# Transformer block of an audio tower on one core: all of W_o's tiles on two-part operands, biases in row groups, two more blocks split

## The reference, cut to what matters

```
h = patches @ W.T + b                        # 64 batches x 10 positions = 640 tokens, D = 512
n = layernorm(h)
q, k, v = n @ Wq.T, n @ Wk.T, n @ Wv.T       # 16 heads of 32, rotary angles on q and k
scores  = q k^T / sqrt(32), causal
heavy   = the key with the largest column sum of softmax(scores)
probs   = softmax(scores where key is heavy or |i - j| <= 1)
h = h + (probs v) @ Wo.T
n = layernorm(h)
h = h + (silu(n @ Wg.T) * (n @ Wu.T)) @ Wd.T # inner width 2048
```

## Time and profile before

| | us |
|---|---|
| median of three runs | 273.25 |
| lowest, highest | 272.64, 273.52 |
| profiled execution, its own time | 272.49 |
| its span, first to last instruction | 270.4 |
| TensorE busy, weight loads busy | 260.1, 215.0 |
| VectorE, ScalarE, GpSimd busy | 169.9, 103.6, 60.0 |

### The profile page before, as it was taken

The page is one execution under the profiler, slowest core; times in us unless marked ns, Lnnn a source line. Parts: engine busy times, 40 slices in busy tenths (PEclk is TensorE's granted clock), DMA queues, the critical chain, the costliest instruction groups (busy, mean ns, idle before and its releaser), DMA issues.

```text
span 270.4 us, 4977 instructions
## 1 busy us (share of the span) xinstructions
PE 260.1 (96%) x1893; PEld 215.0 (80%) x1893; DVE 169.9 (63%) x326; ACT 103.6 (38%) x174; POOL 60.0 (22%) x49
## 2 busy tenths in 40 slices
PE   7999999999899999999989999999999999999993
PEld 5465388893787878687778888999999999999992
DVE  1676998898879976799993864633333333333323
ACT  2211122650274463659531053644333433334320
POOL 0104000002063622103900101322333222222210
PEclk9999999999999999999999999999999999999999
DMA  6995030000048999984493041495333333300004
GB/s 212 421 414 190 15 119 2 2 2 0 0 138 178 327 248 276 281 259 165 152 235 119 1 136 60 123 341 161 116 118 116 116 116 116 127 28 0 0 0 116
DMA packets 12578, 37.51 MB, mean 139 GB/s; under 512 B 1616, under 2 KB 1616, under 8 KB 11920
## 3 DMA queue, kind: packets, MB, share of 16 engines
q1 hardware_dynamic: 11120, 32.15, 34.8%
q0 software_dynamic: 1152, 4.72, 9.2%
q10 hardware_dynamic: 288, 0.39, 0.4%
HBM read 31.23 MB, written 1.31 MB: 120 GB/s over the span
## 4 chain that ended last, share of the span: by engine, by line
PE 68%; DVE 19%; issue 6%; ACT 2%; DMA 2%; POOL 1%; SPq 1%; DVEq 0%; POOLq 0%
PE ps L221 45%; PE ps L1281 5%; PE ps L1300 5%; DVE prod L249 4%; PE ps L1195 3%; PE ps L1103 3%; DVE stats L673 2%; DMA dims<-w_dims 2%; PE ps L1156 1%; PE ps L1125 1%; PE ps L1054 1%; DVE pr L811 1%; PE ps L1135 1%; DVE rowv L809 1%; DVE gu L917 1%
## 5 line engine op out<-in xcount | busy, mean ns | idle before, releaser
L221 PE MATMUL ps<-xT,wgu 128*128 128x384 f32 x384 | 70.5, 339 | 0.1
L221 PEld LDWEIGHTS ps<-xT,wgu 128*128 128x128 f32 x384 | 68.1, 188 | 1.7 <-issue 0.5
L917 DVE TENSOR_TENSOR gu<-silu,ps 128x256 f32<-128x256 f32 (+1 forms) x32 | 15.5, 484 | 50.5 <-PE ps L221 44.4
L358 POOL TENSOR_TENSOR wd<-stage,wd 128x512 fp32r<-128x512 f32 x16 | 26.2, 1637 | 77.1 <-ACT wd L433 77.1
L221 PE MATMUL ps<-wd,hT 128*128 128x512 f32 x156 | 38.8, 393 | 0.0
L572 ACT ACTIVATE silu<-ps 128x256 f32<-128x256 f32 (+1 forms) x32 | 14.1, 440 | 54.5 <-PE ps L221 49.9
L221 PEld LDWEIGHTS ps<-wd,hT 128*128 128x128 f32 x156 | 29.0, 188 | 5.4
L433 ACT ACTIVATE wgu<-stage 128x1024 fp32r<-128x1024 f32 x20 | 21.1, 1056 | 24.0 <-PE ps L221 23.1
L221 PEld LDWEIGHTS ps<-xs,wgu 128*128 128x128 f32 x216 | 25.8, 188 | 3.4 <-issue 1.9
L221 PE MATMUL ps<-xs,wgu 128*128 128x256 f32 x216 | 28.0, 286 | 0.0
L1300 PE MATMUL ps<-stage,gu 128*128 128x512 f32 x56 | 26.5, 595 | 1.2 <-DVE gu L917 1.2
(11 more groups left out here) (122 smaller groups left out, 331.1 us busy)
## 6 DMA issues: line engine op xcount, KB each, us to landing
stage<-w_ffn SPq DMA_DIRECT2D x32, 512.0 KB, 4.3
stage<-w_ffn SPq DMA_DIRECT2D x32, 256.0 KB, 3.7
wgu<-stage POOLq DMA_DIRECT2D x5, 512.0 KB, 7.8
stage<-w_k SPq DMA_DIRECT2D x1, 1024.0 KB, 7.0
stage<-w_q SPq DMA_DIRECT2D x1, 1024.0 KB, 10.5
stage<-w_v SPq DMA_DIRECT2D x1, 1024.0 KB, 12.5
wo<-w_o SPq DMA_DIRECT2D x1, 1024.0 KB, 14.0
wd<-stage POOLq DMA_DIRECT2D x2, 512.0 KB, 7.4
```

The costliest lines, as they stand in the source:

```text
L221: ins = pe.matmul(dst, lhs[a], rhs[b], start=first and n == 0, stop=last and n == 2)
L358: pool.tensor_tensor(dst, src, f32(hi), ALU.subtract).then_inc(done, 1)
L917: dve.tensor_tensor(gu[:, ring, cols], silu[:, ring, cols], ps[:, up, at:at + P * TILES[p]], ALU.mult)\
```

## The change

W_o is loaded into slot 3 of `stage` and split right after the embedding; block 3's load waits until the adding DMA of W_o has landed. The attention of units 0 and 1 gets a low part too (`low_attn(0)`, `low_attn(1)` on VectorE), and `project_out` uses `mm3` for all tiles. `S1` becomes 2, so blocks 2 and 3 of the first pass are split, `hi_whole` and `low_whole` move forward, and `minus_weights(2)` and `(3)` stand around `hi_attn(0)` and `(1)`. The biases of v of group 0 and of all of group 1 are added by products with 8 rows in three row groups (`project_biases`); three GpSimd DMAs for each matrix copy the bias rows there (`spread_bias`). The causal mask goes into one more row of the `place` product, and ScalarE copies the result (`place` on ScalarE). k's third part is projected and rotated later, bias products are moved apart from the tokens they belong to, position 9's reduction is cut in two, the masked softmax has its parts at 4 to 9 and 0 to 3 in place of 0 to 7 and 8 and 9, W_v's bias product is cut in two pieces around `score_place(0)`, v of group 1 is projected between the value sums, and `spread_scale(1)` stands behind the transposes of tile 0. Memory is laid out anew, which adds no instruction.

```diff
-S1, S2 = 4, 11
+S1, S2 = 2, 11
# SP
-            sp.dma_start(wo[:, :, :].rearrange("p k n -> p (k n)"), w_o).then_inc(dma_wo, 16)
+            sp.dma_start(stage[:, 3, :], w_o).then_inc(dma_wo, 16)
...
-            gate_up_load(3)
-            down_load(3)
-            for x in range(3):
+            for x in range(2):
                 sp.wait_ge(fold_bias_mm, x + 1)
                 gate_up_load(x)
                 down_load(x)
+            sp.wait_ge(fold_bias_mm, 3)
+            gate_up_load(2)
+            down_load(2)
+            sp.wait_ge(dma_wo_low, 16)
+            gate_up_load(3)
+            down_load(3)
# GpSimd
+            def spread_bias(x):
+                pool.wait_ge(fold_bias_set, x + 1)
+                for n in range(len(PARTS)):
+                    pool.dma_start(spread[GB * n:GB * n + 2 * NQ, x], fold_bias[0:P:GB // 2, x]).then_inc(dma_spread[x], 16)
...
             key_add(0)
             key_add(1)
+            spread_bias(0)
             key_add(2)
+            spread_bias(1)
+            low_wo()
+            spread_bias(2)
             power(3)
             power(4)
+            low_weights(2)
             power(LN2[1])
+            low_weights(3)
             power(LN2[0])
...
-            low_wo()
# ScalarE
+            def place(n):
+                a, b = CHUNKS[n]
+                act.wait_ge(place_mm, n + 1)
+                if n == 0:
+                    act.wait_ge(sums_set, 2)
+                act.activation(sm[:, a:b].rearrange("p i h j -> p (i h j)"), ps[:, SCORE_BANK[n], 0:HQ * NPOS * (b - a)], ACT.Copy)\
+                   .then_inc(placed, 1)
...
+            folded(2)
             embedded(3)
             embedded(4)
-            folded(2)
-            folded_bias(2)
+            minus_wo()
             chunk_out(0)
+            place(0)
             exponential(0)
             chunk_out(1)
+            place(1)
+            folded_bias(2)
             exponential(1)
...
             act.activation(warm[:, :], neghalf[:, :], ACT.Silu)
+            minus_weights(2)
             hi_attn(0)
             hi_attn(1)
+            minus_weights(3)
             whole_tokens(1)
             whole_tokens(0)
+            hi_whole()
             drain(("v", 1, 0))
-            drain(("v", 1, 1))
-            drain(("v", 1, 2))
# VectorE
             rotate("k", 1)
-            rotate("k", 2)
             bias_join(1)
...
+            rotate("k", 2)
             rotate("q", 2)
             early_products(8)
             early_products(9)
+            dve.wait_ge(product_set, NPOS)
+            step(last_scores(0, 5))
+            softmax_in(0)
+            step(last_scores(5, NPOS))
+            softmax_out(0)
+            softmax_in(1)
             bias_join(2)
-            place(0)
-            softmax_in(0)
-            dve.wait_ge(product_set, NPOS)
-            step(score_reduce(9))
-            softmax_out(0)
-            place(1)
-            softmax_in(1)
             softmax_out(1)
             heavy_keys()
             softmax_in(2)
             softmax_in(3)
             softmax_out(2)
-            values(0, 7, 6, 5, 4, 3, 2, 1, 0)
+            values(0, 7, 6, 5, 4)
             softmax_out(3)
+            low_attn(0)
+            values(0, 3, 2, 1, 0)
             statistics(3)
             statistics(4)
-            token_scale(3)
-            token_scale(4)
+            low_attn(1)
             statistics(LN2[1])
             normalise(LN2[1])
             statistics(LN2[0])
+            token_scale(3)
+            token_scale(4)
             normalise(LN2[0])
             tables(1)
             turn("k", 0)
...
             turn("q", 0)
             first_pass(0)
+            low_whole()
             first_pass(1)
# TensorE
+            def project_biases(x, g):
+                m = "kqv".index(x)
+                pe.wait_ge(pick_set, 1)
+                pe.wait_ge(dma_spread[m], 16 * len(PARTS))
+                for n, (a, b) in enumerate(PARTS):
+                    rows = slice(GB * n, GB * n + 2 * NQ)
+                    dst = ps[:, PROJECT_BANK[PROJECT.index((x, g, n))], 0:DH * (b - a)].rearrange("p (i n) -> p i n", n=DH)
+                    pe.matmul(dst, pick[rows, :], repeated(spread[rows, m], 1, b - a), start=False, stop=True).then_inc(project_mm, 1)
...
+            score_sums(0, ("projection", ("q", 0, 0)))
+            fold_weight_bias(2, 0, 1)
+            score_place(0, ("projection", ("q", 0, 1)))
+            score_sums(1, ("projection", ("k", 0, 2)))
+            fold_weight_bias(2, 2, 3)
+            score_place(1, ("projection", ("q", 0, 2)))
+            project_tokens(("v", 0, 0), ("fold", 2))
+            project_tokens(("v", 0, 1), ("embedding", 3))
+            project_tokens(("v", 0, 2), ("embedding", 4))
+            project_tokens(("k", 1, 0), ("chunk", 0))
+            project_tokens(("k", 1, 1), ("chunk", 1))
+            project_biases("v", 0)
+            project_tokens(("k", 1, 2), ("scores", 0))
+            project_biases("k", 1)
...
+            project_biases("q", 1)
+
+            value_sums(0, ("projection", ("k", 1, 2)))
+            project_tokens(("v", 1, 0), ("fold bias", 2))
+            project_out(1, 1, ("projection", ("k", 1, 0)))
+            value_sums(1, ("projection", ("q", 1, 0)))
+            project_tokens(("v", 1, 1), ("projection", ("v", 0, 2)))
+            project_tokens(("v", 1, 2), ("projection", ("k", 1, 1))).then_inc(tokens_mm, 1)
             project_out(0, 2, ("projection", ("q", 1, 2)))
...
             transposes(LN2[1], ("wo", 1))
-            read_out("projection", ("k", 1, 0))
-            pe.wait_ge(apart_set, NT)
-            spread_scale(1)
+            project_biases("v", 1)
             pe.wait_ge(xf_sb, 1)
             gate_up_whole(0, 1)
             gate_up_whole(1, 1)
             transposes(LN2[0], ("wo", 0))
+            read_out("projection", ("q", 1, 1))
+            pe.wait_ge(apart_set, NT)
+            spread_scale(1)
             pe.wait_ge(xf_sb, 2)
```

More of the change, by code:

```diff
@@ L41 @@
 BIG = 3.4028234663852886e38
+LOWEST = 2.0 ** 127
 CUTS = {"ident": P, "cos": NPOS * HD, "sin": NPOS * HD, "band": NPOS * NPOS, "rank": NPOS, "batch": P, "quad": NQ,
-        "causal": NPOS * NPOS, "quarter": P, "low": 1, "sign": 1, "place": 9 * HQ * NPOS}
+        "quarter": P, "pick": P, "low": 1, "sign": 1, "place": 9 * HQ * NPOS}
 CONSTS = sum(CUTS.values())
@@ L51 @@
 PARTS = [(0, 4), (4, 8), (8, 10)]
-PROJECT = [(x, g, n) for g in range(NG) for x in "kqv" for n in range(len(PARTS))]
-ROTATE = [item for item in PROJECT if item[0] != "v" and item[1] == 0]
+ROTATE = [("k", 0, 0), ("k", 0, 1), ("q", 0, 0), ("q", 0, 1), ("k", 0, 2), ("q", 0, 2)]
+PROJECT = ROTATE + [(x, g, n) for x, g in (("v", 0), ("k", 1), ("q", 1), ("v", 1)) for n in range(len(PARTS))]
 DRAIN = [item for item in PROJECT if item not in ROTATE]
@@ L190, in audio_tower @@
         bias_high, bias_low = sem("bias_high"), sem("bias_low")
+        pick_set, sums_set, dma_spread = sem("pick_set"), sem("sums_set"), [sem(f"dma_spread{n}") for n in range(3)]
         mean_mm, centred_set = sem("mean_mm"), sem("centred_set")
@@ L835, in mask, with low_attn @@
                 step(dve.tensor_tensor(rows(sm, part), rows(sm, part), rows(keep, part), ALU.min))
+            def low_attn(u):
+                a, b = UNITS[u][2]
+                dve.wait_ge(attn_sb, u + 1)
+                dve.tensor_tensor(xT[:, 1, :, columns(u)], ps[:, UNIT_BANK[u], :].rearrange("p (k n) -> p k n", k=KT)[:, :, GB * a:GB * b],
+                                  f32(xT[:, 0, :, columns(u)]), ALU.subtract).then_inc(attn_lo, 1)
             def values(g, *queries):
@@ L978, in _ @@
             scores(1, 3)
-            low_whole()
             turn("q", 1)
@@ L1104, in fold_weight, with fold_weight_bias @@
                 ins.then_inc(fold_mm, 1)
+            def fold_weight_bias(x, *chunks):
                 if x:
                     read_out("fold bias", x - 1)
-                for k in range(KT):
+                for k in chunks:
                     for q in range(NQ):
@@ L1144, in project_parts @@
                     project_tokens((x, g, n), last[n])
-                for n in range(len(PARTS)):
-                    project_bias((x, g, n))
+                project_biases(x, g)
             def score_sums(n, last):
@@ L1165, in score_place @@
                 pe.wait_ge(chunk_sb, n + 1)
-                pe.matmul(ps[:, SCORE_BANK[n], 0:HQ * NPOS * (b - a)], sums[0:rows, n],
-                          cut["place"][0:rows, HQ * NPOS * a:HQ * NPOS * b], start=True, stop=True).then_inc(place_mm, 1)
+                pe.matmul(ps[:, SCORE_BANK[n], 0:HQ * NPOS * (b - a)], sums[0:rows + 1, n],
+                          cut["place"][0:rows + 1, HQ * NPOS * a:HQ * NPOS * b], start=True, stop=True).then_inc(place_mm, 1)
             def spread_scale(g):
@@ L1225, in _ @@
             fold_weight(0)
-            project(("k", 0, 0))
-            project(("k", 0, 1))
```

(11 more changed lines are left out.)

148 lines of the change are left out of this document (65 added, 83 removed).

## The result

The changed kernel takes **277.89 us** (median of four runs, 276.99 to 279.10), the kernel before 273.38 beside it (272.64 to 273.79): a ratio of 1.0172, with a 95% interval of 1.0146 to 1.0199. It is 4.5 us slower where 2.5 were forecast, inside the range given.

What follows compares the result with a forecast made beforehand. TensorE was taken as the bound between 44 and 68 us, with VectorE having 2.6 us to spare. Terms +0.65 + 1.6 + 1.65 - 1.4 = +2.5 us on 273.25 gave 275.8 us, range 272.6 to 278.6.

Steps and rivals of the forecast that it cites:

- Up to the second score product: TensorE up to `score_place(1)`: filled waits and fewer changes between kinds of product make it 1.25 us early.
- The bias copies: First bias triple of v: TensorE waits 1.4 us (0 to 4.5) for GpSimd's DMAs, losing most of the early gain.
- Whatever the size: GpSimd's DMA issue: its instruction takes 0.87 us at any size, so each bias copy was given 0.87.
- The low parts of the attention: Attention to transposes of tile 1: 1.35 us are lost, leaving the second layernorm and normalised tile late by 0.65.
- The tables: Group 1's tables, up to `down_whole(0)`: the later `spread_scale(1)` costs 1.6 us more, making `down_whole(0)` late by 2.25.
- The split of the tokens: `low_whole` ahead of pass 2: GpSimd's value products hold it, about 3.4 us instead of 1.21, costing 1.65 in the sum.
- Two passes shorter: Blocks 2 and 3 of the first pass: 2.74 us each instead of 3.45, giving 1.4 us back.
- From pass 4 on everything keeps its distances: Behind pass 4: nothing but W_o's removed split changes, so lateness there stays the same to the end.
- The rival on the other side (TensorE the bound, faster): Between 44 and 84 us: VectorE's chain gives way and every TensorE saving counts, -5.2 us, 268.1; chance 0.15.

Runs made afterwards that it cites:

- Experiment 1: The changed kernel with the late biases again from the full folded product with the quarter matrix, without the nine bias copies: 275.86 us, ratio 1.0088.
- experiment 2: The changed kernel with SP's load of block 2, and so block 3's behind it, held until the last bias copy landed: 276.29 us, ratio 1.0108.
- experiment 5: The changed kernel with 15 idle identity products put ahead of TensorE's wait for the bias copies: 277.93 us, ratio 1.0177.
- experiment 8: The changed kernel with the edits of experiments 1, 3, 4, six idle products before the first value sums, block 2's copies behind unit 0's: 272.22 us, ratio 0.9979.
- 9: Experiment 8 without the six idle products ahead of the first value sums: 273.05 us, ratio 0.9986.
- experiment 4: The changed kernel with group 1's tables as early as before (statistics scales and spread of the scales moved forward): 276.88 us, ratio 1.0122.
- Experiment 3: The changed kernel with GpSimd's value products of group 0 waiting until VectorE's split of the whole tokens is done: 279.39 us, ratio 1.0227.
- 10: Experiment 8 with tile 4's statistics scale moved into VectorE's wait in the second layernorm of tile 1: 272.25 us, ratio 0.9957.
- 12: Experiment 10 with block 4's adding DMA put between GpSimd's two value products of group 0: 271.64 us, ratio 0.9953.
- 6: The changed kernel with 64 bytes left free ahead of xs in SBUF: 278.78 us, ratio 1.0192.
- 7: The changed kernel with blocks 2 and 3 on whole operands again: 277.79 us, ratio 1.0166.
- 10 to 12: Takes in, between 10 and 12, experiment 8 with blocks 2 and 3 on whole operands: 272.93 us, ratio 1.0007.

## Why the prediction was right, and where it was off

**Up to the second score product:** -1.92 us against a forecast of -1.25. The waits that TensorE's timeline names there shrank from 1.79 us in all to 0.63, by 1.16 where the forecast had 1.0. The rest is 0.76; the forecast had 0.25 there for fewer changes between kinds of product, and no run isolates that term.

**The bias copies** are the term that was mis-sized. I took 2.25 us for the last one, from SP's quiet 64 KB store, and gave 4.1 as the upper bound. The slowest took 4.9. The wait was 3.78 us instead of 1.4, within the bounds of 0 to 4.5: counted from the fold product the first bias triple of v came 1.7 us later than forecast (40.09 instead of 38.4), and TensorE was there 0.7 us sooner. What the working left out is block 3's load. It had block 2's load and W_o's adding DMA beside the copies, but took block 3's, which waits for that DMA and is issued at 45.39 us in the midst of the copies, to cost nothing, since its own use is far off. Experiment 1, which has no copies, puts their price at 2.0 us in the runs (2.6 in the traces), and in experiment 2, which keeps both loads back, 1.6 of it is gone. The issue was the cheaper part: three copies took 1.62 us (44.95 to 46.57), where I had 0.87 each. "Whatever the size" was read from DMAs of 512 KB alone and doesn't hold for these. Behind the copies VectorE waited 2.89 us for the exponential, where the text has 0.9 and its own times, 52.1 less 51.35, give 0.75.

The Trainium skill ("DMA: Bandwidth & Descriptors", anatomy of one DMA on the gpsimd path) gives such a DMA a fixed cost of about 2.0 us. The trace of the changed kernel has 1.5 for the quickest, 3.6 for the median and 4.9 for the slowest, and experiment 2 a median of 2.0 for the last three: that agrees where no load runs beside the copies, and beside one the measurement decides.

**The low parts of the attention** were to leave the transposes of tile 1 0.65 us late; they are 3.40 late. Behind the copies' 1.6 us at the value products (44.90 us from the fold product, forecast 43.33), W_o of tile 1 adds 1.0 (52.01, forecast 49.43). That part the prediction did not have at all, as it had no term for the clock: ScalarE waits 0.88 us for q, whose products ran at the lower clock, and so is late with the copy of unit 0. This is how this trace reads, and not a price: with that stretch filled (experiment 5) q is in time and W_o no sooner, since the clock falls one step later. Where the copies are gone and the wait ahead of the value sums is filled too (8 against 9), the trace gives 1.4 us at these transposes and the runs 0.2 to 0.8, which don't decide it.

**The tables:** +1.71 us from the transposes to `down_whole(0)` (11.69 instead of 9.98), forecast +1.6 (2.25 less 0.65). VectorE's idle time is 1.61 us, forecast 1.9; experiment 4 takes it away.

**The split of the tokens:** the pattern was read rightly from the trace of before: 3.32 us against a forecast of about 3.4, and pass 2 3.19 us behind `down_whole(0)` instead of 1.72: +1.47, forecast +1.65. Experiment 3's trace shows the cause: with GpSimd held back it is 1.22 us.

The Trainium skill ("SBUF — State Buffer", who interferes with whom) has this as a lock of the port pair by whichever engine starts first, and the trace agrees: GpSimd starts at 83.43 us, the split at 83.60.

**Two passes shorter:** -1.09 us up to pass 4 (12.44 instead of 12.06 from `down_whole(0)`, less the 1.47), forecast -1.4. A split pass took 2.87 us where the prediction had 2.74. "From pass 4 on everything keeps its distances" held in the sum, 172.06 us from the value sums to the last products in both kernels, but partly by luck: from pass 4's value sums to group 1's 45 value sums (138.51 us before, 145.51 after) it is 49.24 us instead of 48.63, with split passes that are 0.13 us longer each, and what follows is 0.6 us shorter.

**Sum:** 3.40 + 1.71 + 1.47 - 1.09 = 5.5 us between the two traces without their starts, 4.5 between the medians, forecast 2.5. The forecast's steps were found where it put them, with the copies' term too small and none for the clock. That the time lies inside the range is in part luck: the medians' 4.5 us do, while the traces' 5.5 would have put it just above the upper end, 273.25 + 5.5 = 278.7 against 278.6. The rival on the other side (TensorE the bound, faster) did not come, nor does experiment 8 bring its 268: with the waits gone the time is level with the kernel before.

## What to carry to other kernels

When one engine waits for a tiny DMA, look for what is in flight beside it, and check a load that was moved not only against its own due time but also against what it runs beside: issue the tiny DMA ahead of the large load, keep the load back, or compute the value again. Where several engines are near the limit, shorter products on one of them only open holes, and each step moved to fill them must be checked against the ports, queues and waits of the others. With five such places put right the kernel was level with the one before; it paid, by 0.4 to 0.5%, only with one or two more (experiments 10 and 12), and what paid no longer has the bias copies of the change. When a wait is removed, look at once for the next due time behind it, as with block 4's DMA.

## What the runs showed of the hardware

In the profiled executions idle stretches of TensorE of 3.78 us (the changed kernel), 1.96 (experiment 5), 1.75 (9), 1.74 (1) and even 1.26 (2) were followed by about 3.5 us at half the clock (0.57 to 0.78 granted in the stretches that hold them); in experiments 4, 6 and 7, with waits for the copies of 3.69 to 3.91 us, it was about 7 us. No such fall stands where dummy products kept TensorE busy, in experiment 5 at the first wait and in experiments 8 and 10 to 12 ahead of the value sums. That is no fixed rule: idle stretches of 1.44, 1.55 and 1.24 us in the changed kernel's own trace brought no fall, and some executions of experiments 5 and 9 had a mean clock of 0.999 to 1.00 with the same program. What decides between the two stays open.

Three products with 8 rows each in separate row groups take 0.50 us, where three full ones took 0.84 and one full one alone 0.47: they do run side by side. GpSimd's instruction for a copy of 8 rows takes 0.54 to 0.77 us, for 128 rows 0.87.
